# A gated delta-rule layer: four engines' queues laid out anew, R's last solve moved to the next body, the clip in PSUM

## The reference, cut to what matters

```python
kn = k_t / max(norm(k_t), 1e-12)
pred = S^T kn
r = clip(v_t - pred, -1, 1)
S = a_t[..., None] * S                       # a_t = sigmoid(xn Wa^T + ba), one gate a row
S = S + b_t * kn (v_t - kn^T S)^T            # b_t = sigmoid(xn Wb^T + bb)
o = S^T q_t
R = aR_t[..., None] * R
R = R + g_t * kn (r - kn^T R)^T              # g_t = sigmoid(xn Wg^T + bg)
o = o + R^T q_t
```

## Time and profile before

| what | value |
|---|---|
| median of 3 runs | 2730.33 us (2728.54 to 2733.69) |
| the profiled execution: its time, its span | 2722.71 us, 2720.9 us |
| mean granted PE clock | 0.98 |
| PE busy | 2347.7 us (86%) |
| DVE busy | 1828.2 us (67%) |
| POOL busy | 1304.7 us (48%) |
| ACT busy | 1048.0 us (39%) |
| DMA queue of SP, share of 16 engines | 14.2% |

### The profile page before, as it was taken

How to read it: one execution, slowest core, us unless ns; L and a number is a source line. 1 busy time by engine, 2 the same in 40 slices (tenths; PEclk the granted TensorE clock), 3 DMA queues, 4 the chain that set the end, 5 groups by cost and what they waited for, 6 DMA issues and landing times.

```text
span 2720.9 us, 119181 instructions
## 1 busy us (share of the span) xinstructions
PE 2347.7 (86%) x52544; PEld 1937.0 (71%) x52544; DVE 1828.2 (67%) x3725; ACT 1048.0 (39%) x1552; POOL 1304.7 (48%) x2504
## 2 busy tenths in 40 slices
PE   2999975888888888888888888888888888888887
PEld 2544443777777777777777777777777777777777
DVE  6110116677777777777777777777777777777774
ACT  3222225444443444444444344434444444444330
POOL 0000006455555555555555555555555555555551
PEclk8999987899999999999999999999999999999999
DMA  2000000111111211111111111111112111111111
GB/s 79 0 0 0 0 17 18 37 32 32 29 32 32 43 34 36 34 34 34 34 33 31 42 32 31 30 34 34 34 34 43 34 38 36 33 37 36 35 35 30
DMA packets 306086, 84.74 MB, mean 31 GB/s; under 512 B 280368, under 2 KB 302512, under 8 KB 305584
## 3 DMA queue, kind: packets, MB, share of 16 engines
q1 hardware_dynamic: 305584, 77.25, 14.2%
HBM read 41.53 MB, written 35.65 MB: 28 GB/s over the span
## 4 chain that ended last, share of the span: by engine, by line
PE 45%; DVE 28%; issue 6%; ACT 1%; POOL 1%; DMA 1%; SPq 0%; DVEq 0%; ACTq 0%; POOLq 0%
DVE cum L793 5%; PE bank L453 4%; DVE Kt L816 4%; PE bank L467 4%; DVE AR L842 3%; PE bank L521 3%; DVE rS L887 3%; PE bank L497 3%; PE bank L488 3%; DVE dk L798 3%; PE bank L405 3%; PE bank L578 2%; PE bank L396 2%; PE bank L416 2%; PE bank L411 2%
## 5 line engine op out<-in xcount | busy, mean ns | idle before, releaser
L453 PE MATMUL bank<-kq,Kt 64*64 64x96 f32 x8192 | 354.7, 231 | 3.5 <-DVE kq L832 3.5
L1070 POOL TENSOR_TENSOR lane_x<-lane_x,lane_t 128x15 f32<-128x15 f32 (+7 forms) x960 | 301.3, 314 | 75.2
L453 PEld LDWEIGHTS bank<-kq,Kt 64*64 64x64 f32 x8192 | 309.4, 135 | 8.1 <-DVE kq L832 4.9
L1067 POOL TENSOR_TENSOR lane_t<-lane_n,lane_x 128x15 f32<-128x15 f32 (+7 forms) x960 | 259.2, 270 | 92.7 <-DMA lane_n<-n_dram 13.1
L1017 POOL TENSOR_TENSOR dk<-cum 128x512 f32<-128x512 f32 x64 | 69.7, 1089 | 401.9 <-DVE cum L793 401.9
L1033 POOL TENSOR_TENSOR KQF<-efull,kn 128x768 f32<-128x768 f32 x64 | 117.0, 1829 | 229.3 <-issue 229.2
L553 PE MATMUL bank<-yS,AS 64*64 64x64 f32 x2048 | 134.7, 226 | 102.6 <-DVE Sst L879 102.1
L553 PEld LDWEIGHTS bank<-yS,AS 64*64 64x64 f32 x2048 | 103.9, 134 | 136.6 <-issue 136.6
L1192 ACT ACTIVATE kendT<-bank 128x384 f32<-128x384 f32 x128 | 62.9, 491 | 330.1 <-PE bank L434 321.1
L1084 POOL MEMSET lane_id<- 128x256 f32 x1 | 0.3, 312 | 387.0 <-DVE acc L753 387.0
L1052 POOL TENSOR_TENSOR kend<-Kt,ek 128x768 f32<-128x768 f32 x64 | 95.3, 1489 | 165.9 <-PE bank L434 165.7
(11 more groups left out here) (156 smaller groups left out, 6740.4 us busy)
## 6 DMA issues: line engine op xcount, KB each, us to landing
XF<-x_dram SPq DMA_DIRECT2D x256, 64.0 KB, 2.3
lane_n<-n_dram SPq DMA_DIRECT2D x128, 124.0 KB, 2.8
x_dram<-lane_x SPq DMA_DIRECT2D x128, 124.0 KB, 2.3
n_dram<-AS SPq DMA_DIRECT2D x256, 32.0 KB, 1.7
n_dram<-AR SPq DMA_DIRECT2D x256, 32.0 KB, 1.7
wt<-in_win SPq DMA_DIRECT2D x4, 640.0 KB, 4.6
out_y<-acc SPq DMA_DIRECT2D x16, 128.0 KB, 3.1
hw<-in_h1T SPq DMA_DIRECT2D x1, 1024.0 KB, 7.6
```

Of the source, the lines that this page charges most:

```text
L453: ins = pe.matmul(v3(dst[hd[h], o:o + kinds * C], kinds)[:, :, i * SUB:(i + 1) * SUB], Kt[hd[h], m * 96 + i * SUB:m * 96 + i * SUB + C], r ...
L1067: pool.tensor_tensor(tv, lane_n[:, m * SUB + m + 1:m * SUB + BASE].unsqueeze(2).to_broadcast([L, rows, m + 1]), xv[:, m, 0:m + 1].unsqueez ...
L1070: pool.tensor_tensor(xv[:, m + 1:, 0:m + 1], xv[:, m + 1:, 0:m + 1], tv, ALU.subtract).then_inc(s["lane_step"], 1)
```

## The change

No loop, tile, data type or product changes. The order of the calls in the bodies of PE, DVE, ACT and POOL is new, and with it the waits that must be named:

- PE: `level1_nx` and `level1_zd` of a quad run at the begin of the next body, after or between the projections. Of R, `r_w(3)` and `r_y(3)` follow there, and of S `s_p(3)` and `s_o(3)`; `r_o` runs later for every chunk.
- DVE: `scale_blocks(k+2, 0)`, `mask_products(k+2, 5)` and `scale_blocks(k+2, 1)` stand behind `turn_inverse(k+1)`; before, they stood ahead of it. `s_solved(k+1, 0)` and the first two masks of k+3 stand at the body's end, `own_half` behind `turn_level0`, `operands_k` ahead of `turn_inverse`.
- ACT: the exponentials of the decays open the body; `copy_q` stands ahead of `squares`, `copy_out` behind the logarithms, `copy_v` behind `level0`.
- POOL: `to_end` of a quad runs behind the substitution of the quad before it, instead of ahead of it.
- The clip's first half (v less prediction) is written back to its quarter of bank 5, and the second half reads it there; the tile `rT` is gone. `s_w` and `s_y(0)` wait for the finished clip (`r_sb`) instead of the first half.

DVE around the turn of the inverses, before: AR0 holds the products of quad k+2, Zf0 the inverse of quad k+1, bank5 and bank6 belong to S and R of quad k.

The diff, cut to its core:

```diff
@@ the names of the semaphores @@
-    "kk": "k's operands", "kq": "all operands of the products", ...
+    "kk": "k's operands", "kp": "k's operands of the predictions", "qq": "q's operands", ...
@@ PE @@
             def s_w(n, c):
                 need(pe, "ss_sb", 3 * n + c)
-                need(pe, "sr_sub", 4 * n + c)
+                need(pe, "r_sb", 4 * n + c)
...
             def body(k):
+                if d:
+                    level1_nx(k)
                 if a:
                     project_kq(k + 3)
                 if e:
-                    r_o(k - 1, 3)
+                    s_p(k - 1, 3)
+                    s_o(k - 1, 3)
+                    r_w(k - 1, 3)
...
@@ DVE @@
             def s_clip(n, c):
                 need(dve, "sp_ps", 4 * n + c + 1)
-                dve.tensor_tensor(rT[:, :], vt[n % RING][:, c * P:(c + 1) * P], SB[:, 3 * P:4 * P], ALU.subtract).then_inc(s["sr_sub"], 1)
+                left = SB[:, 3 * P:4 * P]
+                dve.tensor_tensor(left, vt[n % RING][:, c * P:(c + 1) * P], left, ALU.subtract).then_inc(s["sr_sub"], 1)
                 need(dve, "sr_sub", 4 * n + c + 1)
-                dve.tensor_scalar(rS[c % 2][:, :], rT[:, :], 1.0, -1.0, ALU.min, ALU.max).then_inc(s["r_sb"], 1)
+                dve.tensor_scalar(rS[c % 2][:, :], left, 1.0, -1.0, ALU.min, ALU.max).then_inc(s["r_sb"], 1)
...
@@ DVE's body, around the turn @@
                 if l:
                     turn_inverse(k + 1)
                 if d:
-                    s_solved(k, 2)
                     r_state(k, 1)
                     s_state(k, 2)
-                if a:
-                    own_half(k + 3)
+                if b:
+                    scale_blocks(k + 2, 0)
+                    mask_products(k + 2, 5)
                 if d:
                     s_clip(k, 2)
                     r_right(k, 2)
-                if a:
-                    operands_k(k + 3)
+                if b:
+                    scale_blocks(k + 2, 1)
...
@@ POOL @@
             def body(k):
-                if on(k + 1):
+                b, l = on(k + 2), on(k + 1)
+                if l:
+                    to_end(k + 1)
+                if b:
+                    far(k + 2)
+                    against_state(k + 2)
+                    far_half(k + 2)
+                if l:
                     small_inverses(k + 1)
-                if on(k + 3):
-                    far(k + 3)
-                    against_state(k + 3)
-                    far_half(k + 3)
-                    to_end(k + 3)
@@ ACT @@
             def body(k):
                 a, b, l, d, e = on(k + 3), on(k + 2), on(k + 1), on(k), on(k - 1)
-                if a:
+                if b:
+                    from_anchor(k + 2)
+                    from_begin(k + 2)
+                    to_anchor(k + 2)
+                if d:
+                    level0(k)
+                if b:
+                    copy_v(k + 2)
+                if l:
+                    copy_kend(k + 1)
+                if d:
+                    level1(k)
+                if a:
+                    copy_q(k + 3)
                     squares(k + 3)
...
```

More of the change, by code:

```diff
@@ L71 @@
     "kdiag": "K^ of the own half", "kfar": "K^ of the first half for the second",
-    "kk": "k's operands", "kq": "all operands of the products", "kf": "k against the state", "ea1": "one over S's gate", "kfull": "operands against the state",
+    "kk": "k's operands", "kp": "k's operands of the predictions", "qq": "q's operands", "kf": "k against the state", "ea1": "one over S's gate", "kfull": "operands against the state",
     "kend": "k decayed to the chunk's end", "kT_ps": "turned in PSUM (2)", "kT_sb": "turned in SBUF (2)",
@@ L562, in r_w @@
                 need(pe, "ry_sb", 4 * n + c)
+                need(pe, "kfull", n + 1)
                 for p in range(2):
@@ L618, in body @@
                 if e:
-                    r_o(k - 1, 3)
+                    s_p(k - 1, 3)
+                    s_o(k - 1, 3)
+                    r_w(k - 1, 3)
+                if d:
+                    level1_zd(k)
+                if a:
+                    project_a(k + 3)
+                if e:
+                    r_o(k - 1, 2)
+                if b:
+                    products(k + 2, 0)
                 if d:
@@ L622, in body @@
                 if b:
-                    products(k + 2, 0)
-                if a:
-                    project_a(k + 3)
+                    products(k + 2, 1)
                 if d:
                     s_s(k, 0)
-                    s_o(k, 0)
-                if b:
-                    products(k + 2, 1)
                 if a:
                     project_r(k + 3)
+                if e:
+                    r_y(k - 1, 3)
                 if d:
@@ L636, in body @@
                     products(k + 2, 2)
+                    products(k + 2, 3)
                 if d:
+                    r_y(k, 0)
                     s_w(k, 1)
-                    r_y(k, 0)
-                if b:
-                    products(k + 2, 3)
                 if a:
                     norms(k + 3)
+                if e:
+                    r_o(k - 1, 3)
                 if d:
                     s_y(k, 1)
-                    r_s(k, 0)
-                    r_o(k, 0)
                 if b:
                     products(k + 2, 4)
+                    products(k + 2, 5)
                 if d:
+                    r_s(k, 0)
+                    s_o(k, 0)
                     s_s(k, 1)
-                    s_o(k, 1)
-                if b:
-                    products(k + 2, 5)
+                if a:
+                    project_v(k + 3)
                 if d:
@@ L661, in body @@
                     s_w(k, 2)
+                    s_o(k, 1)
                     r_y(k, 1)
-                if a:
-                    project_v(k + 3)
-                if d:
                     s_y(k, 2)
-                    r_s(k, 1)
-                    r_o(k, 1)
+                    r_o(k, 0)
                 if l:
@@ L672, in body @@
                     s_s(k, 2)
+                    r_s(k, 1)
                     s_o(k, 2)
+                    r_o(k, 1)
+                    r_w(k, 2)
                     s_p(k, 2)
-                    r_w(k, 2)
                 if l:
@@ L685, in body @@
                     r_s(k, 2)
[L686 to L696, removed]
             for k in range(-3, LAST + 2):
@@ L951, in body @@
                 if d:
-                    r_state(k, 0)
+                    s_solved(k, 1)
                 if a:
@@ L958, in body @@
                     s_state(k, 1)
-                if b:
-                    mask_products(k + 2, 5)
-                    scale_blocks(k + 2, 1)
+                    r_state(k, 0)
                 if a:
@@ L998, in body @@
                 if a:
[L999 removed]
+                    operands_q(k + 3)
                 if d:
                     s_clip(k, 3)
[L1002 removed]
+                if a:
+                    operands_prev(k + 3)
                 if l:
@@ L1005, in body @@
                 if d:
-                    r_solved(k, 3)
+                    r_right(k, 3)
+                if l:
+                    s_solved(k + 1, 0)
+                if a:
+                    mask_products(k + 3, 0)
+                    mask_products(k + 3, 1)
             for k in range(-3, LAST + 2):
```

80 lines of the change are left out of this document (34 added, 46 removed).

## The result

The changed kernel is slower, and the forecast of 2640 us was wrong. Its median is 2836.17 us (2826.26 to 2848.27, 4 runs) beside 2729.43 us (2727.31 to 2733.69, 4 runs) of the kernel before on the same chip: ratio 1.0392, 95% interval 1.0373 to 1.0411. The profiled execution took 2826.26 us, its span is 2824.4 us at a mean granted clock of 0.909; before it was 2720.9 at 0.98.

What follows compares the result with a forecast made beforehand. Before was taken as bound by PE's and VectorE's queue order, afterwards by the inverses' trip: 20.7 + 13.0 = 33.7 us for 61 periods, 31.1 for the last two, giving 2640 us; 8-in-10 range 2525 to 2740.

Steps and rivals of the forecast that it cites:

- R: GpSimd's substitution in the trip of the inverses, partly stretched by VectorE's running sums: taken as 13.0 us, bounds 10.4 and 14.04.
- The loop of the sum: Trip of the 16-wide inverses, from one XF landing to the next: 20.7 us plus 13.0 of substitution, 33.7 us a period.
- PE's order: Large products cover S and R results: no PE wait over 0.3 us except at level0_nx; PE work 30.9 us or less.
- X to scale 1 done: From XF's landing through level0_nx, the states, scale 0, mask 5 and clip to the end of scale 1: 6.1 us.
- AR's issue to the lanes' issue: SP's issuing of AR's DRAM writes and the wait for them, before the lanes' read is issued: 3.7 us.
- lanes' issue to first step: From the issue of the lanes' read to GpSimd's first substitution step: 3.5 us.
- XF's issue to turn: From the issue of the XF read to its use in turn_inverse: 3.65 us.
- the gap ahead of AR's issue: From the end of scale 1 to SP's first issue for AR: 0.4 us.
- the inverses' way: From the issue of the inverses' write to DRAM to XF's issue: 3.3 us.
- the last two periods: End of the run, where no running sums meet the substitution: 10.43 us of substitution, 31.1 us a period.
- the slower one: Unhidden DRAM trip exceeds the old period, turn_inverse and level0_nx waiting for XF: 35.9 us a period, +46, 2776 us; chance 0.11.
- The clip: First half written to PSUM on VectorE: taken as 0, bounds -0.77 and +0.4 us a body.

Runs made afterwards that it cites:

- the extra microsecond: One 128x512 GpSimd product added between lanes' landing and first substitution step: 2917.9 us in the changed kernel, 2526.9 us in that with scales before turn_inverse.
- the scales ahead: Changed kernel with both scales and mask 5 of quad k+2 put back ahead of turn_inverse(k+1), directly behind r_state(k, 0): 2513.4 us.
- The extra products: Changed kernel with unused 128x512 PE products added right ahead of level0_nx: 2812.3 us with four, 2803.67 us with six.
- the move alone in the kernel before: Kernel before with only both scales and mask 5 of quad k+2 moved behind turn_inverse(k+1) and the states: 2865.69 us, ratio 1.0509.

## Why the prediction was wrong, by its own steps

*Right: what bounds after.* XF's landing ends PE's wait (26 of some 27 quads, 4.2 us each, a little above the 2 to 4 forecast) and VectorE's (2.9); GpSimd waits 11.5 us for the lanes (8 to 12); the waits of s_p and s_y are gone; steps beside the running sums take 1.09 and 1.29 us; R is 12.84 (12.5 to 13.5). The loop of the sum is the loop of the trace, term by term, and the extra microsecond bears it out.

*Right: PE's order.* The forecast took 30.9 us of PE work or less as what is late next where the loop is not. With the scales ahead the period is 31.74, of which PE is busy 0.9395 x 31.74 = 29.8.

*Wrong, and it decided: "X to scale 1 done", 6.1 us.* It took 8.18, 2.08 us more in each period. The term was priced at the clock of before: `level0_nx` 1.84 us; it took 3.00 on average. But the same forecast had PE wait 2 to 4 us ahead of exactly this product. In the row at 1501.32 it waited 5.75 us, the clock was 0.54, and its two halves took 3.43 us up to the next product at 1504.75. The forecast's own wait was enough for that: in the 27 quads in which PE waited 2 to 4 us, the mean clock over `level0_nx` was 0.66 to 0.78. The extra products show the share of the clock: 1.95 us, counted from the start of `level0_nx`. At the full clock the way is then 6.34, close to the 6.1 of the sum, so the steps were listed rightly and priced at the wrong clock. The rest is small: scale 0 is at times blocked by GpSimd (from 1000 to 2000 us 0.82 us on average against 0.69, up to 1.78). The sum named bounds for R and the clip, and none for this term. It decided the sign, by estimate: 36.67 less 2.08 is 34.6, below the 35.05 of before.

*Wrong by less.* AR's issue to the lanes' issue (+0.39), lanes' issue to first step (+0.29), XF's issue to turn (+0.73, of it 0.4 by the three bodies in which PE waited for weights and the turn was late, which the sum did not see). Against them: R -0.16, the gap ahead of AR's issue -0.26, the inverses' way -0.10. Together with the 2.08 that is +2.97 us: 36.67 instead of 33.7, and 63 x 2.97 = 187 of the 194 us between forecast (-90) and measured (2824.4 - 2720.9 = +103.5). Another 5 are the last two periods, forecast at 31.1 and measured at 34.0 and 33.4.

*The rival that came true* is the slower one, by its place (turn and `level0_nx` waiting for XF) and its point (over 35.05 us), at 0.11. Its price of 35.9 fell short of the 36.67, and its reasons were in part others: it wanted R at 14.04 and 0.6 us more on each DRAM wait. R stayed at 12.84, the legs through DRAM gave 1.3 together (0.4 of it the late turns), and the clock, which it did not name, gave the most. The sum left 1.35 us to the point where the sign turns, in a loop in which every term is paid 63 times; with seven terms and so small a margin, 0.85 for faster was too much.

*The clip,* taken at 0, is -0.26% in the old order and nothing in the new. *The Trainium skill's* rule (SBUF — State Buffer, Who interferes with whom) says that a VectorE instruction with two SBUF inputs contends with a GpSimd instruction that reads SBUF. The row at 1525.32 agrees: beside a running sum GpSimd's step took 1.29 us against 0.29; the scales at 1528.07 and 1529.68 show it the other way round.

## What to carry to other kernels

Before a producer step is moved behind the consumer of the same pipeline's last round, write down the loop that this closes, and price it against the period, at the clock that the loop's own wait will leave. If the margin is below the spread of its terms, keep the producer ahead: here its place alone was 2836 against 2513 us. Then look at what the moved step runs beside and what waits behind it: the same steps, also ahead but later, gave 2789. To find out whether a trip is the bound, put a known microsecond in it and see whether it comes back once per period (1.3 us) or not (0.2).

## What the hardware showed that was not expected

- Around the end of one idle time of PE of 5.75 us, in a stream busy for 88%, 5 us stand at a granted clock of 0.54 and the next 5 at 0.78, though PE's busy share hardly differs from before; behind one of 2.62 us (the move alone in the kernel before) a 5 us piece shows 0.50. Before, where PE's waits of rows 3 reach 1.5 us at most, the 500 us stretch shows 1.00.
- The terms of this loop do not move alone. By the profiles, 1.25 us off one term (six extra PE products) moved the period by 0.46, with PE then nearly full; 0.93 put into another moved it by 1.43.
- A VectorE product of 0.69 us took 1.69 and 2.29 beside GpSimd's 128x768 steps; GpSimd's 128x55 step of 0.29 (1520.40) took 1.29 beside a running sum of 1.23. In the rows at 1525.31 and 1525.32, and at 1527.39 and 1528.07, the one that started later is the one that is stretched; at 1529.17 and 1529.68 both are. No run isolated that.
